# Loads of one row group over 128 partitions in place of loads of 32 partitions, in a two-layer graph network kernel

## The reference

```
h = relu(layernorm(x))
t0 = h; t1 = adj @ t0; t2 = 2 adj @ t1 - t0; t3 = 2 adj @ t2 - t1
x = x + t0 W0 + t1 W1 + t2 W2 + t3 W3            # 64 x 64 weights
h = relu(layernorm(x))
deg = clip(sum(adj, axis=1) + 1, 1)
z = concat(h, (adj @ h + h) / deg) @ W + b
out = relu(z); out = out / max(norm(out), 1e-12)
x = x + out
```

## Time and profile before

| | |
|---|---|
| median of three runs | 2900.0 us |
| the profiled execution | 2887.5 us |
| its span, first to last instruction | 2885.2 us |
| TensorE busy | 2197.4 us (76%) |
| VectorE busy | 1636.7 us (57%) |
| ScalarE busy | 678.3 us (24%) |
| GpSimd busy | 828.5 us (29%) |
| moved by the DMA engines | 690.24 MB, 239 GB/s over the span |
| mean granted clock of TensorE | 0.884 |

### The profile page before, as it was taken

The page is one execution under the profiler, slowest core; times in us unless marked ns, Lnnn a source line. Parts: engine busy times, 40 slices in busy tenths (PEclk is TensorE's granted clock), DMA queues, the critical chain, the costliest instruction groups (busy, mean ns, idle before and its releaser), DMA issues.

```text
span 2885.2 us, 30932 instructions
## 1 busy us (share of the span) xinstructions
PE 2197.4 (76%) x12008; PEld 1690.3 (59%) x12008; DVE 1636.7 (57%) x1306; ACT 678.3 (24%) x1667; POOL 828.5 (29%) x1593
## 2 busy tenths in 40 slices
PE   2478878869999898885498877868656968886676
PEld 1245556656777777774477655656545747653444
DVE  5477666646565555643344455554453666686677
ACT  1332332223223325211112243411111112200000
POOL 2222322122232353111121442422114232244250
PEclk9689989989999989997798888889878989998787
DMA  9699999699999969876579876976679989999996
GB/s 252 197 300 300 306 297 303 176 278 272 267 268 268 271 167 264 226 211 160 157 205 237 221 201 168 255 200 164 185 195 274 249 234 276 306 322 291 251 254 139
DMA packets 246868, 690.24 MB, mean 239 GB/s; under 512 B 69058, under 2 KB 85698, under 8 KB 246722
## 3 DMA queue, kind: packets, MB, share of 16 engines
q1 hardware_dynamic: 140096, 345.09, 44.9%
q0 software_dynamic: 101632, 341.94, 42.3%
q10 hardware_dynamic: 4994, 1.25, 0.3%
HBM read 685.97 MB, written 2.10 MB: 238 GB/s over the span
## 4 chain that ended last, share of the span: by engine, by line
PE 41%; DMA 24%; ACT 11%; DVE 9%; SPq 8%; issue 4%; POOL 2%; ACTq 0%; DVEq 0%; POOLq 0%
PE ps_pair L783 29%; DMA ring<-in_adj_dram 24%; ACT ring L425 10%; PE ps_single L789 8%; SPq L354 7%; DVE ring L635 7%; POOL ring L379 2%; SPq L339 1%; PE ps_lin L725 1%; PE ps_lin L728 1%; PE ps_single L687 1%; DMA res<-in_x_dram 0%; PE ps_tr L744 0%; PE ps_lin L727 0%; PE ps_xt L677 0%
## 5 line engine op out<-in xcount | busy, mean ns | idle before, releaser
L635 DVE STREAM_TRANSPOSE ring<-ring 128x2048 f32<-128x2048 f32 (+1 forms) x680 | 1431.6, 2155 | 1085.4 <-ACT ring L425 846.0
L783 PE MATMUL ps_pair<-ring,vec 128*128 128x256 f32 x5760 | 1374.5, 401 | 382.5 <-DVE ring L635 367.5
L783 PEld LDWEIGHTS ps_pair<-ring,vec 128*128 128x128 f32 x5760 | 1147.9, 202 | 596.7 <-issue 226.5
L379 POOL DMA_DIRECT2D ring<-in_adj_dram x1584 | 827.5, 531 | 1989.2 <-PE ps_pair L783 915.7
L789 PE MATMUL ps_single<-ring,vec 128*64 128x256 f32 x4480 | 596.1, 420 | 274.2 <-DVE ring L635 269.1
L425 ACT ACTIVATE ring<-ring 128x1024 f32<-128x1024 f32 (+7 forms) x736 | 574.6, 783 | 814.4 <-DMA ring<-in_adj_dram 631.4
L789 PEld LDWEIGHTS ps_single<-ring,vec 128*64 128x64 f32 x4480 | 338.6, 150 | 499.6 <-issue 191.6
L448 ACT ACTIVATE sum_s<-ps_single 128x512 f32<-128x512 f32 x64 | 37.8, 591 | 497.0 <-PE ps_single L789 344.7
L425 ACT ACTIVATION_READ_ACCUMULATOR ring<-ring 128x1 f32 x736 | 138.5, 188 | 0.0
L460 ACT ACTIVATE stat<-stat 128x4 f32<-128x4 f32 x16 | 3.3, 205 | 267.1 <-DVE stat L583 267.1
L436 ACT ACTIVATE vec_t<-ps_xt 64x512 f32<-64x512 f32 x32 | 18.6, 583 | 181.4 <-PE ps_xt L677 181.4
(11 more groups left out here) (94 smaller groups left out, 582.0 us busy)
## 6 DMA issues: line engine op xcount, KB each, us to landing
ring<-in_adj_dram SPq DMA_DIRECT2D x752, 256.0 KB, 17.0
ring<-in_adj_dram POOLq DMA_DIRECT2D x752, 256.0 KB, 16.7
ring<-in_adj_dram POOLq DMA_DIRECT2D x176, 224.0 KB, 16.8
ring<-in_adj_dram SPq DMA_DIRECT2D x176, 224.0 KB, 22.9
ring<-in_adj_dram SPq DMA_DIRECT2D x160, 128.0 KB, 13.4
ring<-in_adj_dram POOLq DMA_DIRECT2D x160, 128.0 KB, 9.2
ring<-in_adj_dram SPq DMA_DIRECT2D x80, 192.0 KB, 17.0
ring<-in_adj_dram POOLq DMA_DIRECT2D x80, 192.0 KB, 11.1
```

Of the source, the lines that this page charges most:

```text
L379: pool.dma_start(strip_of(i)[32 * a:32 * a + 32, ar:GH:Q, :], adj_v[ar, :, at:at + CB // H, col:col + w * UC]).then_inc(s_high[i % NSEM], 16)
L635: last = nc.vector.transpose(blocks, blocks)
L783: last = nc.tensor.matmul(ps_pair[n % 2][:, cells], vec[:, CB * J + c, :, :], moving, start=(pair == 0), stop=(pair == pairs - 1))
```

## The change

Each load now takes one group `g` over all 128 partitions: four column quarters times 32 matrix rows, which is 128 runs. SyncE issues the four even groups of a strip, GpSimd the four odd ones. The view of `adj` is cut anew, so that the two axes of a load's source that are not columns are `a` (the column quarter, count 4, the outer one) and `r` (the row, count 32). The semaphores are renamed, and `loaded` counts four loads per queue in place of eight. The bytes, the runs, their lengths, the strips, the ring and all waits stay.

```
-    adj_v = adj.rearrange("(a c r) m -> a r c m", a=Q, r=32)
+    adj_v = adj.rearrange("(b c r) (a m) -> b c a r m", b=Q, r=32, a=Q)
...
-            return 16 * 2 * Q * (i // NSEM + 1)
+            return 16 * (GH // 2) * (i // NSEM + 1)
...
@@ SyncE
-                for ar in range(Q):
-                    for a in (0, 1):
-                        col = a * QN + J0 * UC
-                        sp.dma_start(strip_of(i)[32 * a:32 * a + 32, ar:GH:Q, :],
-                                     adj_v[ar, :, at:at + CB // H, col:col + w * UC]).then_inc(s_low[i % NSEM], 16)
+                for g in range(0, GH, 2):
+                    src = adj_v[g % Q, at + g // Q, :, :, J0 * UC:J0 * UC + w * UC]
+                    sp.dma_start(strip_of(i)[:, g, :], src).then_inc(s_even[i % NSEM], 16)
...
@@ GpSimd
-                for ar in range(Q):
-                    for a in (2, 3):
-                        col = a * QN + J0 * UC
-                        pool.dma_start(strip_of(i)[32 * a:32 * a + 32, ar:GH:Q, :],
-                                       adj_v[ar, :, at:at + CB // H, col:col + w * UC]).then_inc(s_high[i % NSEM], 16)
+                for g in range(1, GH, 2):
+                    src = adj_v[g % Q, at + g // Q, :, :, J0 * UC:J0 * UC + w * UC]
+                    pool.dma_start(strip_of(i)[:, g, :], src).then_inc(s_odd[i % NSEM], 16)
```

More of the change, by code:

```diff
@@ L304, in cheb_sage_kernel @@
         s_wready = sem("weights_ready")
-        s_low = [sem(f"strip_low_loaded{i}") for i in range(NSEM)]
-        s_high = [sem(f"strip_high_loaded{i}") for i in range(NSEM)]
+        s_even = [sem(f"strip_even_loaded{i}") for i in range(NSEM)]
+        s_odd = [sem(f"strip_odd_loaded{i}") for i in range(NSEM)]
         s_turned = sem("units_turned")
@@ L417, in sum_rows @@
                     lo, hi = row.summed(i - first_strip[n])
-                    act.wait_ge(s_low[i % NSEM], loaded(i))
-                    act.wait_ge(s_high[i % NSEM], loaded(i))
+                    act.wait_ge(s_even[i % NSEM], loaded(i))
+                    act.wait_ge(s_odd[i % NSEM], loaded(i))
                     if row.sweep > 1 and extra_rows.index(n) >= 2:
@@ L617, in _ @@
                     seen.add(i)
-                    dve.wait_ge(s_low[i % NSEM], loaded(i))
-                    dve.wait_ge(s_high[i % NSEM], loaded(i))
+                    dve.wait_ge(s_even[i % NSEM], loaded(i))
+                    dve.wait_ge(s_odd[i % NSEM], loaded(i))
                     if i in sum_strips:
```

## The result

The changed kernel takes 6044 us (four runs, 6041 to 6154) where the one before takes 2899 us on the same chip: 2.085 times as long, 95% interval 2.081 to 2.089. Now and then a run of any of these kernels comes out a per cent or two slow, as the 6154 us did, and the times and ratios here leave such runs out. The forecast was 5278 us with a range of 4300 to 7200. The direction and the main mechanism held; the time was 15% over the forecast.

The account below looks back on a forecast made before the run. TensorE (41% of the chain) and DMA loads (24%) co-bound the kernel; after the change, four engines' loading does. 5.7 + 5215 (106.9 MB at 20.5 GB/s) + 42 = 5263 us, plus 2.3 and 12.5, gives 5278 us; range 4300 to 7200.

Parts of the forecast that it names:

- the main mechanism: SyncE's new loads fall on four DMA engines while GpSimd's spread over 16, so loading sets the pace; chance 0.83.
- How many engines: Each new load, its source leading with 4, runs on four DMA engines; q1 then shows 117920 packets, not 127424.
- Which engines: SyncE's loads always use the same four engines, GpSimd's spread over all 16; each busy engine carries 106.9 MB.
- Which half is late: In each strip SyncE's even half always comes last; GpSimd's loads land clearly earlier.
- The speed of one engine: Each of the four busy engines moves 20.5 GB/s, so its 106.9 MB take 5215 us; ends 4568 and 7097 us.
- slow end: On the four engines, GpSimd's 21.4 MB and as much of SyncE's at 18.8 GB/s, 64.1 MB at 13.3: 7097 us.
- Rival D: The main forecast with the loading engines held at 13.3 GB/s: 7160 us; its chance is included in the forecast's 0.83.
- What hides the rest: TensorE's 2197 us, VectorE's 1637, ScalarE's 678 and the epilogues lie under loading; only 5.7 and 42 us stay outside.
- Smaller parts: Halved loads free 339 us of SyncE's and 419 us of GpSimd's issue time, worth nothing; fewer signals save no time.
- Rival A: All 16 engines carry each load over all 128 partitions: faster, 2632 us at best, 2760 us taken; chance 0.10.
- Rival B: Both queues' loads fall on the same four engines, 171 MB each at 20.5 GB/s: 8404 us; chance 0.04.
- Rival C: All 16 engines carry loads, but both queues' packets meet on the same partitions: 2885 to 2900 us; chance 0.03.

## Why the prediction was right, and what was off

**How many engines.** Right, to the packet. The step from "the bias ran on one engine" to "a source that leads with 4 runs on four" was a choice between 1 and 16; the runs with 2, 8 and 128 show it as a rule. The Trainium skill (DMA: Bandwidth & Descriptors, "Why a DMA increments its semaphore by 16 and not by 1") states it, and the packets agree with it in every count that was run: 2, 4, 8, 32 and 128 on q1, and 1 (the bias) on q10.

**Which engines.** SyncE's loads stayed on the same four: while q1 is alone four of its runs are in flight, the 24.5%, although its queue is full; loads that went to other engines would run beside one another. GpSimd's spread over all, by the runs in flight. The share that each engine carries is not in the trace, which does not name engines, so that one of the four has 106.9 MB is borne out and not measured: 311 MB, or 78 MB for each of four, went while three to five runs were in flight.

**Which half is late.** This step was wrong in part. The prediction had the even half of a strip always last and GpSimd's landings clearly earlier. GpSimd's half was last in 79 of the 198 strips, though by 3 us only. Its loads are issued 42 us before SyncE's in the median, but they share the four engines, and there its packets, those of a few bytes too, take turns with SyncE's, as in the stretch above. That this is what holds its landings back was not tested by a run of its own. The pace is still that of the four engines. The page has other marks as well than were written: a DMA share of mostly 4 to 6 tenths in place of 2 to 4, since GpSimd's slow packets keep 16 engines occupied, 114 GB/s in place of near 130, and a chain that has loads and their issue for 74%, not almost all.

**The speed of one engine.** This is the term that was mis-sized. The prediction took 20.5 GB/s for all 106.9 MB. An undisturbed engine gives 25.5, above the 23.4 that was the fast end. But GpSimd's part is much slower than any row of before: 36.6% of 6042.5 us is 2212 us per engine for 21.4 MB, 9.7 GB/s, where the sum took 20.5 and its slow end 18.8. SyncE's 18.8% over four engines is 4544 us for 85.5 MB, 18.8 GB/s, undisturbed for 208 MB and held up for the rest. The two sum to 6756 us, more than the span, so GpSimd's packets on these four take less than their mean. The trace shows this: of its 55168 packets of 4096 bytes, whose mean is 374 ns, 8274 went while three to four runs were in flight and took 164 ns. All told, 106.9 MB in the 5995 us between the two ends of the sum are 17.8 GB/s in place of 20.5. The "two of them may get in each other's way" of the slow end was the right worry in the wrong place: SyncE's four go at full rate side by side, and it is 16 at a time that disturb one another. Rival D was priced too low for what it says: 7160 us hold only 64.1 MB at 13.3 GB/s, and all 106.9 MB at that rate would be 8100 us, outside the range.

**What hides the rest.** Nearly right. For some 225 us no run is in flight, where the sum left 48 us outside the loading. TensorE, ScalarE and VectorE still hold 24% of the chain; how much of that the loads would have filled with longer queues was not tried.

**Smaller parts.** That fewer issues are worth nothing holds by two runs: here, and with 32 partitions x 4 groups, where half the loads made 0.7% more. Signals cost nothing on q1. On q0 the change adds some 212000 packets of 4 to 32 bytes (237216 against 25344 before) that the prediction did not have; at 11 to 13 ns each on average they are some 150 us more of each of the 16 engines. What they cost by holding back GpSimd's landings no run tells apart.

**Rival A** was priced for what another kernel does, and too low at that. With the count of engines kept at 16 the same destinations are worth 11% (2568 us), more than the 2632 us taken as the best. The prediction priced the DMA part of the chain at 357 GB/s; the loads went at 402, and DMA fell from 24% to 15% of the chain. The Trainium skill (SBUF — State Buffer, "Door 1: The DMA port swizzle") has it that the partitions 0 to 63, which are SyncE's half, reach half the ports. That is borne out: 213 GB/s of one queue before, 16 engines at about 310 ns per 4096 bytes, twice the 160 of an engine alone. Its rule that only a span over 128 partitions reaches all 16 ports fits the 402 against 301 GB/s, but doesn't give the 301 by itself, since the two queues before cover all partitions between them. **Rival B** is out by the time and by GpSimd's spread. **Rival C** would need 16 engines.

**Why 16 engines are slow in GpSimd's bursts** is shown only in part. The trace gives the mean time of a 4096-byte packet by the number of runs in flight at the time, of both queues together:

| | 3 to 4 | 7 to 8 | 11 to 12 | 15 and more |
|---|---|---|---|---|
| changed kernel, GpSimd's | 164 ns | 276 ns | 351 ns | 444 ns |
| changed kernel, SyncE's beside GpSimd's | 163 ns | 224 ns | 355 ns | 435 ns |
| leading with 8, GpSimd's | | 168 ns | 271 ns | 351 ns |
| leading with 128, GpSimd's | | | | 163 ns |

So it is not the queue, nor the shape of a load alone: with four in flight GpSimd's packets go at full rate, and with 16 both queues' are equally slow. It is hardly the reading side, and not the span over 128 partitions (402 GB/s). What remains is that the four shares of a load walk the same positions of their quarters, and four loads do so at a time, so that up to 16 engines meet on a few ports. That fits every run, but it was argued: a load that leads with 4 and starts elsewhere can't be built for the same strip, and wasn't tried.

None of the correct versions that were run beats the one before. The gain of the kernel that leads with 128 needs a source with one count over the partitions, and a strip holds the same 32 matrix rows in four column quarters: to be one count, the second quarter would have to lie 32 rows after the first, and it lies in the same row.

## What to carry to other kernels

Look at the outermost count of both sides of a transfer before its size: the largest number up to 16 that divides both is the number of DMA engines that it gets (the runs here tried powers of two alone), and on SyncE's and ScalarE's queues the packets of the row, less the runs, over the number of transfers, tell it from any profile. A span over 128 partitions pays only if the source leads with a large count as well (11% won here with 128, 40% lost with 8); where it can't, give each queue a fixed half of the partitions, and don't let both roam over all (9 to 13% lost here). An issue instruction that suddenly takes microseconds is a full queue, not an issue cost.

## What the runs showed of the hardware that was not expected

- One DMA engine moves 25.5 GB/s with rows of 4 KB (160 ns each) and keeps that rate beside 15 others, 402 GB/s in all, in the kernel whose loads lead with 128. The 301 GB/s of the kernel before were no limit of the memory.
- A transfer of GpSimd's that runs on fewer than 16 engines adds packets of a few bytes: 237216 for 792 loads that lead with 4, 87680 for leading with 8, 12672 (16 per load) for 128.
- On an engine that two queues share, the 4-byte packets of the one take turns with the packets of the other, nearly all of 4096 bytes (203 beside 203 in eight microseconds). GpSimd's half strips, issued 42 us before SyncE's in the median, still landed last in 79 of 198 cases, and the chain of waits names such a landing "unknown".
- SyncE's issue is held up to 52.8 us when its engines are behind.
